# Projecting a node table from unnormalised rows with centred weights, three steps behind the attention loop

## The reference, cut to what matters

```python
x = x + _L1_gnn_ref(_layernorm(x), adj, L1_gnn_W, L1_gnn_a, L1_gnn_bias)      # third layer: graph attention
x = x + _L1_ffn_ref(_layernorm(x), ..., W_gat, att_src, att_dst, ..., edge_index)   # fourth layer

# in the fourth layer, over all 16384 nodes:
h = x_flat @ W_gat                          # 128 features to 16 columns
a_src = (h * att_src).sum(-1)               # 4 columns
a_dst = (h * att_dst).sum(-1)               # 4 columns
e = leaky_relu(a_src[src] + a_dst[dst])     # for 524288 edges
```

## Time and profile before

| | us |
|---|---|
| median of 3 runs | 3086.28 (3086.01 to 3090.51) |
| time of the profiled execution | 3091.0 |
| its span on the core | 3088.6 |
| attention loop of layer 3 with its tail | about 1305 to 1640 |
| busy over the span: DVE, POOL, PE, ACT | 2253.5, 1843.8, 1796.8, 1204.5 |

### The profile page before, as it was taken

How to read it: one execution, slowest core, us unless ns; L and a number is a source line. 1 busy time by engine, 2 the same in 40 slices (tenths; PEclk the granted TensorE clock), 3 DMA queues, 4 the chain that set the end, 5 groups by cost and what they waited for, 6 DMA issues and landing times. The chain is left out here.

```text
span 3088.6 us, 31245 instructions
## 1 busy us (share of the span) xinstructions
PE 1796.8 (58%) x8829; PEld 1241.0 (40%) x8829; DVE 2253.5 (73%) x4422; ACT 1204.5 (39%) x2447; POOL 1843.8 (60%) x1723
## 2 busy tenths in 40 slices
PE   0676764308888888375874244565446554565445
PEld 0555653305555555265773122232223322333223
DVE  7999978698899999887754456555665556655566
ACT  2576674514444444065872122222222222222222
POOL 5600024773445444377676777777777777777772
PEclk9899885559999999588876677877777776777777
DMA  5697000110111110222111121222122211222111
GB/s 214 211 356 295 4 18 22 39 36 24 34 49 40 47 43 13 69 77 77 28 38 39 39 41 34 42 44 42 31 42 44 45 42 31 42 44 42 37 39 36
DMA packets 170130, 192.35 MB, mean 62 GB/s; under 512 B 59241, under 2 KB 126096, under 8 KB 169008
## 3 DMA queue, kind: packets, MB, share of 16 engines
q1 hardware_dynamic: 107616, 118.69, 11.5%
q0 software_dynamic: 57088, 62.48, 10.0%
q10 hardware_dynamic: 5328, 9.97, 0.9%
HBM read 91.70 MB, written 105.25 MB: 64 GB/s over the span
## 5 line engine op out<-in xcount | busy, mean ns | idle before, releaser
L1523 POOL DMA_INDIRECT edge_rows<-node_table,edge_ids x1024 | 996.8, 973 | 313.2 <-issue 296.5
L1148 POOL DMA_INDIRECT token_results<-arena,token_of x160 | 249.3, 1558 | 301.2 <-ACT arena L1084 221.3
L585 DVE TENSOR_TENSOR sort_ping<-sort_pong 128x1024 f32<-128x1024 f32 (+1 forms) x232 | 395.2, 1745 | 12.6 <-ACT sort_pong L1018 8.1
L1141 POOL DMA_INDIRECT slots<-arena,send x128 | 174.9, 1366 | 376.2 <-ACT arena L1040 340.8
L585 DVE TENSOR_TENSOR sort_pong<-sort_ping 128x1024 f32<-128x1024 f32 (+1 forms) x230 | 390.0, 1736 | 8.6 <-ACT sort_ping L1018 3.7
L1646 PE MATMUL x_b_featT<-ident,x_feat 128*128 128x128 f32 x128 | 34.8, 427 | 619.6 <-PEq L1245 619.6
L1393 DVE TENSOR_TENSOR win_score<-win,masked 128x320 f32<-128x320 f32 x64 | 28.7, 490 | 446.4 <-DMA win<-edge_table,win_ids 445.2
L1652 PE MATMUL x_b_hid<-x_featT,x_w 128*128 128x512 f32 x512 | 311.0, 762 | 28.3 <-PEq L1245 28.3
L1659 PEld LDWEIGHTS x_b_res<-x_w,x_hid 128*128 128x128 f32 x2048 | 246.8, 197 | 97.1 <-issue 97.1
L1646 PEld LDWEIGHTS x_b_featT<-ident,x_feat 128*128 128x128 f32 x128 | 22.9, 217 | 625.0 <-issue 625.0
L1659 PE MATMUL x_b_res<-x_w,x_hid 128*128 128x128 f32 x2048 | 271.8, 288 | 0.0
(11 more groups left out here) (348 smaller groups left out, 4214.8 us busy)
## 6 DMA issues: line engine op xcount, KB each, us to landing
edge_table<-zeros SPq DMA_DIRECT2D x8, 5120.0 KB, 35.7
edge_rows<-node_table,edge_ids POOLq DMA_INDIRECT x1024
arena<-slots SPq DMA_DIRECT2D x40, 260.0 KB, 2.6
slots<-zeros SPq DMA_DIRECT2D x2, 5120.0 KB, 24.4
edge_table<-edge_rows SPq DMA_DIRECT2D x64, 160.0 KB, 2.1
out_dram<-x_y ACTq DMA_DIRECT2D x33, 256.0 KB
x<-in_x_dram SPq DMA_DIRECT2D x4, 2048.0 KB, 16.2
adjacent<-in_adj_dram SPq DMA_DIRECT2D x32, 256.0 KB, 2.7
```

What stands on the lines that cost most here:

```text
L585: step(dve.tensor_tensor(vb[:, :, t, :], va[:, :, 0, :], va[:, :, 1, :], op))
L1141: pool.indirect_dma_start(slots_dram, bass.IndirectOffsetOnAxis(send[:, q:q + 1], 0), sent_feat[:, n % 2, v, :], None, bounds_check=EXPERT ...
L1148: pool.indirect_dma_start(rows_dram, bass.IndirectOffsetOnAxis(token_of[:, n % 4, r:r + 1], 0), res[:, n % 2, r, :], None, bounds_check=TO ...
L1523: pool.indirect_dma_start(rows[:, u, c, :], None, table_dram, bass.IndirectOffsetOnAxis(ids[:, u, c:c + 1], 0)).then_inc(rows_in[u], 16)
```

## The change

The rows of `x` go through the projection as they are. Since `(x - mean) @ W` is `x` times `W` with the mean of each column taken off, the weights are centred once: PE sums the columns of `gat_w` with a matrix of ones, and DVE takes 1/128 of the sums off. The factor `rstd` of a row is multiplied into the table afterwards, a quarter at a time, by a new DVE instruction (128x768 elements). ACT's normalising for the projection is gone (four instructions a group), and `feat` with it. `LAG` goes from 12 to 3. PE turns a group two steps ahead of its product, ACT copies the turned rows as its first instruction in a step, and DVE keeps a group one step later than PE projects it. SP's store of a quarter waits for the scaling.

```diff
 class Projection:
...
-    def act_step(self, act, n, u):
-            a, f = n + 1, n + 2
+    def act_step(self, act, a, u):
             if live(a):
                 act.wait_ge(self.turned, a + 1)
                 ge(act, self.projected, a - 1)
...
-            if live(f):
-                ge(act, self.turned, f - 1)
-                normalise(act, self.feat[:, u % 2, :, :], self.x, self.rstd, self.shift, f).then_inc(self.normed, 1)
 
     def pe_step(self, pe, n, u):
-            a = n + 1
+            a = n + 2
             if live(a):
-                pe.wait_ge(self.normed, a + 1)
-                ge(pe, self.featT_s, a - self.ahead + 1)
+                pe.wait_ge(self.updated, a + 1)
+                ge(pe, self.featT_s, a)
...
             if live(n):
                 pe.wait_ge(self.featT_s, n + 1)
-                ge(pe, self.kept, n - self.ahead + 1)
+                ge(pe, self.kept, n)
...
-    def dve(self, dve, n):
-        dve.wait_ge(self.projected, n + 1)
...
+    def dve_keep(self, dve, n):
+        if live(n):
+            dve.wait_ge(self.projected, n + 1)
+            dve.tensor_scalar(self.into[:, n * PER:(n + 1) * PER, :], self.b_out[:, :, 0:self.cols], 1.0, None, ALU.mult).then_inc(self.kept, 1)
+
+    def dve_scale(self, dve, c, chunk, rstd):
+        part, each = self.into[:, c * chunk * PER:(c + 1) * chunk * PER, :], rstd.unsqueeze(2).to_broadcast([P, chunk * PER, self.cols])
+        dve.wait_ge(self.kept, (c + 1) * chunk)
+        dve.tensor_tensor(part, part, each, ALU.mult).then_inc(self.scaled, 1)
...
-        LAG, CHUNK = 12, GROUPS // 4
...
+        LAG, CHUNK = 3, GROUPS // 4
...
+            dve.wait_ge(gat_summed, 1)
+            dve.scalar_tensor_tensor(gat_w[:, :], b_centre, -1.0 / FEAT, gat_w[:, :], ALU.mult, ALU.add).then_inc(gat_made, 1)
...
-                if n >= LAG:
-                    gat.dve(dve, n - LAG)
+                gat.dve_keep(dve, n - LAG - 1)
+                if n > CHUNK and n % CHUNK == LAG:
+                    dve.wait_ge(gat_norms[n // CHUNK - 1].done, n // CHUNK)
+                    gat.dve_scale(dve, n // CHUNK - 1, CHUNK, gat_norms[n // CHUNK - 1].rstd)
...
-            for n in range(GROUPS + 1 - LAG, GROUPS):
-                gat.dve(dve, n)
-                if n % 3 == 0:
-                    search()
+            for n in range(GROUPS - LAG, GROUPS):
+                gat.dve_keep(dve, n)
+            dve.wait_ge(gat_norms[-1].done, GROUPS // CHUNK)
+            gat.dve_scale(dve, GROUPS // CHUNK - 1, CHUNK, gat_norms[-1].rstd)
...
-                sp.wait_ge(gat.kept, (c + 1) * CHUNK)
+                sp.wait_ge(gat.scaled, c + 1)
...
             for n in range(-3, GROUPS + LAG):
                 att1.pe_step(pe, n, n % 4)
-                gat.pe_step(pe, n - LAG, n % 4)
+                gat.pe_step(pe, n - LAG, (n - LAG) % 4)
...
             for n in range(-4, GROUPS + LAG):
+                gat.act_step(act, n - LAG + 1, (n - LAG + 1) % 4)
                 att1.act_step(act, n, n % 4)
...
-                gat.act_step(act, n - LAG, n % 4)
```

More of the change, by code:

```diff
@@ L353, with __init__ @@
 class Projection:
[L354 to L360, removed]
-    def act_step(self, act, n, u):
-            a, f = n + 1, n + 2
+    def __init__(self, sem, tag, x, updated, ident, weight, cols, into, featT, b_featT, b_out):
+        self.turned, self.featT_s, self.projected, self.kept, self.scaled = (
+            sem(f"{tag}_{n}") for n in ("turned", "featT", "projected", "kept", "scaled"))
+        self.x, self.updated, self.ident, self.weight, self.cols, self.into = x, updated, ident, weight, cols, into
+        self.featT, self.b_featT, self.b_out = featT, b_featT, b_out
+    def act_step(self, act, a, u):
             if live(a):
@@ L366, in act_step @@
                 ge(act, self.projected, a - 1)
-                act.activation(self.featT[:, (u + 1) % 2, :, :], self.b_featT[(u + 1) % 2][:, :, :], ACT.Copy).then_inc(self.featT_s, 1)
-            if live(f):
-                ge(act, self.turned, f - 1)
-                normalise(act, self.feat[:, u % 2, :, :], self.x, self.rstd, self.shift, f).then_inc(self.normed, 1)
+                act.activation(self.featT[:, u % 2, :, :], self.b_featT[:, :, :], ACT.Copy).then_inc(self.featT_s, 1)
     def pe_step(self, pe, n, u):
-            a = n + 1
+            a = n + 2
             if live(a):
-                pe.wait_ge(self.normed, a + 1)
-                ge(pe, self.featT_s, a - self.ahead + 1)
+                pe.wait_ge(self.updated, a + 1)
+                ge(pe, self.featT_s, a)
                 for v in range(PER):
-                    last = pe.transpose(self.b_featT[(u + 1) % 2][:, v, :], self.feat[:, (u + 1) % 2, v, :], self.ident)
+                    last = pe.transpose(self.b_featT[:, v, :], self.x[:, a * PER + v, :], self.ident)
                 last.then_inc(self.turned, 1)
@@ L381, in pe_step @@
                 pe.wait_ge(self.featT_s, n + 1)
-                ge(pe, self.kept, n - self.ahead + 1)
+                ge(pe, self.kept, n)
                 for v in range(PER):
-                    last = pe.matmul(self.b_out[u % 2][:, v, 0:self.cols], self.featT[:, u % 2, v, :], self.weight, start=True, stop=True)
+                    last = pe.matmul(self.b_out[:, v, 0:self.cols], self.featT[:, u % 2, v, :], self.weight, start=True, stop=True)
                 last.then_inc(self.projected, 1)
-    def dve(self, dve, n):
-        dve.wait_ge(self.projected, n + 1)
-        dve.tensor_scalar(self.into[:, n * PER:(n + 1) * PER, :], self.b_out[n % 2][:, :, 0:self.cols], 1.0, None, ALU.mult).then_inc(self.kept, 1)
+    def dve_keep(self, dve, n):
[6 more added lines that the diff above has]
+        dve.tensor_tensor(part, part, each, ALU.mult).then_inc(self.scaled, 1)
 def front(nc, sem, a, x, x_in, stats, scratch, rstd, shift, masked, tab, W, fills, ident, ones, upto, row_id, wanted, counted, found,
@@ L468, in front @@
             "step", "less", "exp", "chosen", "ranked", "placed", "order", "done"))
-        LAG, CHUNK = 12, GROUPS // 4
-        gat = Projection(sem, "gat", x, rstd, shift, ident, gat_w[:, :], TAB, tab, view, banks, 4112, (1, 1), (3, 3))
+        LAG, CHUNK = 3, GROUPS // 4
+        b_centre = banks[:, 3, 0:TAB]
+        gat_summed = sem("gat_summed")
+        gat = Projection(sem, "gat", x, att1.updated, ident, gat_w[:, :], TAB, tab, view(4112, 2, PER, NODES),
+                         banks[:, 1, :].rearrange("p (v i) -> p v i", v=PER), banks[:, 3, :].rearrange("p (v i) -> p v i", v=PER))
         gat_norms = []
@@ L1007, in _ @@
             pe.wait_ge(gat_made, 2)
+            pe.matmul(b_centre, ones[:, :], gat_w[:, :], start=True, stop=True).then_inc(gat_summed, 1)
+            pe.wait_ge(gat_made, 3)
             for n in range(-3, GROUPS + LAG):
                 att1.pe_step(pe, n, n % 4)
-                gat.pe_step(pe, n - LAG, n % 4)
+                gat.pe_step(pe, n - LAG, (n - LAG) % 4)
         @block.scalar
```

## The result

The changed kernel takes 3144.25 us (median of four runs, 3140.37 to 3145.82), the kernel before 3086.15 beside it: a ratio of 1.0184, with a 95% interval of 1.0166 to 1.0201. That is 58 us slower; 44 were forecast. The profiled execution took 3145.82 us, with a span of 3143.5. The second function takes 1447 us behind the barrier, as it did (1448), and the first step of the attention loop starts at 1329.99 (1330.67 before), so all of the loss lies in that loop.

The account below looks back on a forecast made before the run. DVE's searches, fed by POOL's fetches and held up by the projection's tail, bound the stage's end. Search 21 59 us later, less POOL's 10.0 and the tail's 5.1, gave +44: 3130 us, range 3106 to 3151 (81%).

Parts of the forecast that it names:

- The wait and its sign: PE's product waits on single bank 3 for DVE's late keep in nearly every step from 4; slower, 0.86.
- The step of the ring: PE and DVE taking turns through bank 3: 8.9 us a step with joining, 7.4 without; together 30 us.
- The ring in the norms' steps: Attention-loop steps with layer norms got no price of their own; steps were priced only as with or without joining.
- The clock: PE at half speed behind its new idle times: 2.4 us in twelve early steps, 1.0 in thirteen late ones.
- search 21: DVE search in step 29 that POOL's batch 28 waits for: 30 + 16 + 13 = 59 us later.
- What the old loop paid: Seven of old steps 5 to 16 start L252 at half speed, costing 13 us, taken off the new clock cost.
- POOL's slack: POOL's batch 28 starts 10.0 us after search 21 ends; only delay beyond that moves the end.
- The tail: Projection's keeps on DVE after the loop: 5.1 us at the stage's end, gained by dropping nine of twelve steps.
- PE at its full clock all through: Rival: no half speed in the loop, so +2 us, 3088, the same within measurement; chance 8%.
- The second, 3081: Rival: DVE reaches the keep in time, the wait is covered and the tail's 5.1 us go; chance 6%.
- The rule named there: Skill's rule on a second PSUM buffer, cited for the 3081 rival: the single bank would cost nothing here.
- The scaling of a quarter: New DVE instruction on 768 elements a row, four in all: 0.7 to 1.0 us each, taken as hidden.

Follow-up runs that it names:

- seven turns: Changed kernel with PE turning the same rows seven times (groups up to 15) or three times (later) ahead of the product's wait: 3114.07 us, ratio 1.0091.
- keep ahead of joining: Changed kernel with the late keep behind L296 and L98 but ahead of joining and layer norms on DVE: 3096.84 us, ratio 1.0035.
- experiments 1: Changed kernel with DVE keeping group n-3 instead of n-4 in step n, the step of its product: 3088.3 us, ratio 1.0007.
- 2: Changed kernel with the keep still a step late, but as DVE's first instruction in the step: 3088.32 us, ratio 1.0007.
- 4: Kernel before with only the keep made one step later (group n-13 in step n): 3124.5 us, ratio 1.0128.

## Why the prediction was right, and where it was off

The lengths of some steps, as differences of the starts of L271 (us):

| step | before | after | seven turns | keep ahead of joining | keep in the same step |
|---|---|---|---|---|---|
| 7 (joining, search) | 7.87 | 10.80 | 9.13 | 9.24 | 8.70 |
| 9 (joining, norm) | 10.90 | 15.09 | 12.29 | 10.02 | 9.48 |
| 17 (norms) | 9.71 | 15.12 | 15.49 | 9.82 | 9.21 |
| 18 (behind them) | 7.47 | 10.58 | 10.87 | 6.54 | 6.53 |
| 23 (late) | 6.53 | 7.62 | 7.63 | 7.62 | 6.53 |
| 25 (norm) | 8.46 | 12.87 | 11.25 | 10.01 | 8.47 |
| 26 (behind it) | 6.54 | 9.30 | 9.30 | 7.22 | 6.54 |
| 4 to 28 together | 214.4 | 278.0 | 247.0 | 232.8 | 214.6 |

- **The wait and its sign: right.** The product waits for DVE's keep 28 times, 71.7 us in all. Undoing the place of the keep alone (experiments 1, 2) gives the old time, and making it alone (4) gives 39 of the 58 us, with the old tail ending the stage.
- **The step of the ring: right at an equal clock, where its legs were priced.** 8.9 was worked out with joining and 7.4 without; 9.13 and 7.6 were measured with PE filled.
- **The ring in the norms' steps: left out.** At an equal clock the prediction has 30 us, less the 13 that the old loop lost at half speed: +17 over steps 4 to 28. With seven turns it is 247.0 - 214.4 = +32.6. Steps 17, 18, 25 and 26 make 14.7 of that, against 13 / 13, or 1.0, a step in the prediction. The norms stand ahead of the keep, and they wait for ACT. That was to be read in the order on DVE, which the front part names. But not all of the 14.7 is the ring. In steps 17, 18 and 26 PE was still at half speed, behind pauses of 2.54, 3.61 and 2.69 us, and these steps are no shorter with the seven turns than without. PE behind the pause of 3.61 us, and one step later at full speed:

```profile
1510.12 1.88 PE L378 MATMUL banks<-gat_w,arena 128*128 128x24 f32 x8 [3.61 <-DVE masked L384]
1511.82 1.09 PE L221 MATMUL banks<-ident,arena 128*128 128x128 f32 x4
...
1519.02 1.47 PE L372 MATMUL banks<-ident,x 128*128 128x128 f32 x12
1520.99 1.04 PE L378 MATMUL banks<-gat_w,arena 128*128 128x24 f32 x8 [0.50 <-DVE masked L384]
...
1526.65 1.47 PE L372 MATMUL banks<-ident,x 128*128 128x128 f32 x12
```

From the product to the turn behind it, 8.90 us pass and then 5.66. By like differences in the three steps some 8 of the 14.7 are half speed, an estimate; that leaves about +24.5 for the ring, against +17.

- **The clock: near its price.** It was priced at 29 early and 13 late, 42. Steps 4 to 28 of the changed kernel less those with seven turns are 31.0: 23 in steps 4 to 17, 8 in the later ones. With the 8 that the turns did not give back it is some 39. For search 21, 59 was worked out and 64.8 came; by this estimate the ring is what was priced too low, and the clock a little too high.
- **What the old loop paid: read too high.** Seven of its steps 5 to 16 do start L252 at half speed, but three only in part (1.75, 1.46 and 1.57 us in place of 2.06). By the rows of L252 and L264 it is about 10.5 and not 13, so that the +17 would have been +19.5. And an idle time such as was expected now did not always lead there: step 8 starts L252 at full speed behind 3.00.

```profile
1391.61 1.13 PE L252 MATMUL banks<-arena 128*128 128x129 f32 x8 [3.00 <-DVE x L279]
...
1420.54 1.46 PE L252 MATMUL banks<-arena 128*128 128x129 f32 x8 [3.00 <-DVE x L279]
```

- **POOL's slack: right.** 10.0 was taken off; 64.8 - 56.0 = 8.8 came off.
- **The tail: the step that failed.** "So 5.1 us at the end belong to the tail" took DVE to be what ends the stage. DVE did gain them: its end moved by 50.0 while the fetch moved by 56.0. The stage did not. POOL comes to the barrier 9.2 us behind its last fetch (1638.4 in the kernel before, as late as DVE), so the 5.1 were never to be had. What comes behind the barrier on POOL, before:

```profile
1640.61 0.29 POOL L1505 TENSOR_SCALAR_AFFINE_SELECT column_end<-ones 128x128 f32<-128x128 f32 x1 [11.42 <-POOLq L1690]
```

Without that term the sum would have been +49; +55.9 was measured in the profiled loop.

- **The rivals.** PE at its full clock all through was priced at 3088; with the clock forced up over most of the loop it is 3114, some 8 us of which are half speed still left. The rest above 3088 is the ring, dearer than thought. The second, 3081, fell twice: the wait is not covered, and the tail gives nothing back. The rule named there (the Trainium skill, TensorE: Matmul & The Clock Gate, section HAM oscillation: a second PSUM buffer brought one kernel nothing further) would have made the single bank free of cost. The traces agree with it where the keep stands early (experiments 1 and 2, 1.0007), and not where it stands late (58 us). What decides is the place of the keep, which reads the bank, in DVE's step.
- **What was not tried.** Two halves of bank 3 in turn would be the plain second buffer. The Trainium skill, PSUM — Partial Sum Buffer, section PSUM bank collisions raise a hardware error, says that two engines may not use the same bank at once; no run here shows it, and the loop uses all eight banks.

The scaling of a quarter was put at 0.7 to 1.0 us; it took 0.96, in the last quarter behind a keep that waited 2.06 us for PE:

```profile
1666.16 0.26 DVE L384 TENSOR_SCALAR masked<-banks 128x96 f32<-128x96 f32 x1 [2.06 <-PE banks L378]
1666.52 0.96 DVE L389 TENSOR_TENSOR masked<-masked,rstd 128x768 f32<-128x768 f32 x1
```

## What to carry to other kernels

When a producer waits for a single buffer to be emptied, look where in the emptying engine's step that instruction stands: add up all that stands ahead of it there, waits for third engines included, because from then on it lies in one ring with the producer's own step. Moving the emptying instruction to the front of its step gave back the 58 us here, to within what a measurement can tell. And before a gain at the end of a stage is booked, find which engine comes to the barrier last: freeing an engine that merely ends at the same time was worth nothing here.

## What the runs showed of the hardware

POOL's sequencer closes its block 9.23 us behind the end of its last gather: its closing record in the trace, which the timeline leaves out, ends at 1638.42 against 1629.19 before, at 1694.42 against 1685.19 after, and the distance is the same 9.23 in the profiles of all the experiments. The gather's own landing is 2.4 us, so this is not the data's arrival alone. What it consists of stays open. In the table above it sets the stage's end wherever DVE is not later.
